# Routing of a two-expert MoE block by sums of powers of two, with row numbers counted on TensorE, and a jump-back hint held in a register

## The reference

```python
h = _layernorm(x) * (1 + ca) + sa
g = sigmoid(h @ Wg.T + bg);  a = sigmoid(h @ Wd.T + bd);  v = h @ Wv.T + bv
x = x + ga * (scan(h_t = a_t * h_{t-1} + (1 - a_t) * v_t) * g)
h = _layernorm(x) * (1 + cb) + sb
probs = softmax(h @ gate_w.T + gate_b);  top 2 of 8 -> dense_gate
y_e = relu(h @ w1[e] + b1[e]) @ w2[e] + b2[e]
x = x + gb * sum_e dense_gate[e] * y_e
```

## Time and profile before

| | |
|---|---|
| median of 3 runs | 443.9 us (442.91 to 444.16) |
| the profiled execution | 442.52 us, of which the span is 440.7 us |
| busy, share of the span | DVE 88%, PE 83%, ACT 73%, POOL 43% |
| mean granted clock of TensorE | 0.922 of full speed |
| chain that ended last, by engine | PE 58%, DVE 27%, issue 8% |

### The profile page before, as it was taken

The page is one execution under the profiler, slowest core; times in us unless marked ns, Lnnn a source line. Parts: engine busy times, 40 slices in busy tenths (PEclk is TensorE's granted clock), DMA queues, the critical chain, the costliest instruction groups (busy, mean ns, idle before and its releaser), DMA issues.

```text
span 440.7 us, 15289 instructions
## 1 busy us (share of the span) xinstructions
PE 366.2 (83%) x4679; PEld 316.8 (72%) x4680; DVE 386.4 (88%) x1099; ACT 320.0 (73%) x992; POOL 188.7 (43%) x213
## 2 busy tenths in 40 slices
PE   1859889789787683489999999999999999999660
PEld 1435555456455562489999999999999999989660
DVE  4989999989998999699999899999999998888660
ACT  1445999688979550188988888889888888877530
POOL 8023303376678477884333243333333334324321
PEclk9986999989999655599999999999999999999895
DMA  7813643131223243563333333333333333232200
GB/s 217 223 48 106 202 146 106 48 128 73 92 90 126 93 163 147 147 197 106 84 98 84 95 94 100 87 88 86 87 86 91 94 85 87 66 81 73 64 11 7
DMA packets 45941, 45.27 MB, mean 103 GB/s; under 512 B 5934, under 2 KB 40575, under 8 KB 45874
## 3 DMA queue, kind: packets, MB, share of 16 engines
q1 hardware_dynamic: 38208, 27.28, 23.1%
q0 software_dynamic: 6592, 16.92, 10.6%
q10 hardware_dynamic: 1074, 0.23, 0.3%
HBM read 24.52 MB, written 20.81 MB: 103 GB/s over the span
## 4 chain that ended last, share of the span: by engine, by line
PE 58%; DVE 27%; issue 8%; DMA 2%; ACT 1%; SPq 1%; POOL 0%; POOLq 0%; ACTq 0%; DVEq 0%
PE bank L1513 8%; PE bank L1514 8%; PE bank L1515 8%; PE bank L1530 8%; PE bank L1531 7%; PE bank L1529 7%; DVE xn L921 3%; PE bank L1526 2%; DVE hs L935 2%; PE bank L1488 2%; PE bank L1370 2%; DVE st L865 2%; DVE u L931 2%; DVE st L859 2%; DVE pay L944 2%
## 5 line engine op out<-in xcount | busy, mean ns | idle before, releaser
L755 ACT ACTIVATE xs<-bank,b1col 128x128 f32<-128x128 f32 x624 | 165.2, 415 | 26.4 <-PE bank L1515 25.5
L590 POOL DMA_INDIRECT out_dram<-tg,midx x78 | 81.9, 1049 | 150.9 <-DVE tg L1299 135.0
L1513 PE MATMUL bank<-xh,w1hi 128*128 128x128 f16 x624 | 109.9, 223 | 6.6 <-issue 3.7
L1529 PE MATMUL bank<-w2hi,xs 128*128 x624 | 112.7, 219 | 0.0
L1530 PE MATMUL bank<-w2hi,w2f 128*128 x624 | 112.6, 219 | 0.0
L1531 PE MATMUL bank<-w2lo,xs 128*128 x624 | 112.6, 219 | 0.0
L1515 PE MATMUL bank<-xh,w1lo 128*128 128x128 f16 x624 | 109.9, 222 | 0.0
L1514 PE MATMUL bank<-xl,w1hi 128*128 128x128 f16 x624 | 109.9, 223 | 0.0
L1279 DVE TENSOR_TENSOR w2f<-xs 128x1024 f16<-128x1024 f32 x78 | 95.6, 1225 | 2.7
L561 POOL DMA_INDIRECT sorted_rows<-pay,idx x64 | 69.1, 1080 | 28.2 <-issue 18.7
L1277 DVE CAST xs<-xs 128x1024 f16<-128x1024 f32 x78 | 54.7, 701 | 13.1 <-ACT xs L755 9.5
(11 more groups left out here) (232 smaller groups left out, 654.2 us busy)
## 6 DMA issues: line engine op xcount, KB each, us to landing
xs<-sorted_rows SPq DMA_DIRECT2D x78, 130.0 KB
xs<-sorted_rows SPq DMA_DIRECT2D x78, 64.0 KB
sorted_rows<-padt SPq DMA_DIRECT2D x5, 582.0 KB, 5.3
w2f<-in_L_ffn_w_dram SPq DMA_DIRECT2D x4, 512.0 KB, 3.9
xs<-in_L_ffn_w_dram SPq DMA_DIRECT2D x4, 512.0 KB, 3.8
xs<-in_L_attn_x_dram SPq DMA_DIRECT2D x3, 512.0 KB, 8.7
out_dram<-tg,midx POOLq DMA_INDIRECT x78
sorted_rows<-pay,idx POOLq DMA_INDIRECT x64, 2.7
```

The lines of the kernel that those rows point to most:

```text
L590: pool.indirect_dma_start(out_rows, bass.IndirectOffsetOnAxis(midx[k][:, t:t + 1], 0), yout[k][:, t, :], None, bounds_check=TOK - 1, oob_i ...
L755: ins = act.activation(hf[e][:, cc, t * P:(t + 1) * P], bank[2 * e + cc // 2][:, o:o + P], ACT.Relu, bias=b1col[:, bass.ds(ex[t][e] * HC + ...
L1513: pe.matmul(o, whi, xh[n % 2][:, rows], start=True, stop=False)
L1529: pe.matmul(o, hh[n % 2][e][:, cc, rows], whi, start=False, stop=False)
```

## The change

Routing: the two choices are coded as powers of two (`desc` holds 128, 64, ..., 1 in place of 8, 7, ..., 1). Their sum `key` names the pair, and `OH` compares it with a table `key_of`. The arithmetic that made a pair's number, its direction and its start (`cmax`, `cmin`, `elo`, `tri`, `q`, `aq`, `way`, `start`) goes. PE's count adds the start of each list by one more matmul with `list_base`, and takes backward and forward lists in separate matmuls of 14 lists each, the former with negative masks; the product with `OH`, summed, is the row number itself. POOL's setup makes the new tables. The loop is written by hand: a register `final` is 1 in the last turn and 0 before, and the prefetch hint takes its outcome from it.

```diff
+        @contextmanager
+        def tile_loop(eng, turns):
...
+            nc.regs_mov(it, PEEL)
+            nc.br(head, engines=on)
+            with nc.body(head, valid_engines=on):
+                now = nc.snap(it, min_val=PEEL, max_val=MAX_TURNS - 1)
+                eng.reg_alu(final, now + 1, turns, ALU.is_ge)
+                place = eng.mark_branch_hint_location()
+                yield now
+                nc.regs_alu(it, it, 1, ALU.add)
+                eng.br_lt(it, turns, on_true=head, on_false=behind).branch_hint(place, final)
+            nc.switch_bb(behind)
...
-            with nc.Fori(PEEL, turns, engines=[pe.engine], hint_back_edge=True) as it:
+            with tile_loop(pe, turns) as it:
...
-            mark(pool.iota(cnti[:, E:2 * E], pattern=[[-1, E]], base=E, channel_multiplier=0))
+            for e in range(E):
+                mark(pool.memset(desc[:, e:e + 1], float(1 << (E - 1 - e))))
+            mark(pool.memset(list_base[:, :], 0.0))
...
+                mark(pool.tensor_scalar(key_of[:, first:first + hi], desc[:, 0:hi], float(1 << (E - 1 - hi)), None, ALU.add))
...
-                mark(dve.tensor_tensor(m["cmax"], m["c1"], m["c2"], ALU.max))
-                mark(dve.tensor_tensor(m["cmin"], m["c1"], m["c2"], ALU.min))
-                done = marked(dve.tensor_tensor(m["isl"], m["c1"], m["c2"], ALU.is_gt))
-                yield
-
-                dve.wait_ge(dve_step, done)
-                mark(dve.tensor_scalar(m["elo"], m["cmax"], -1.0, E * (E - 1) / 2 + E - MID, ALU.mult, ALU.add))
-                done = marked(dve.scalar_tensor_tensor(out=m["tri"], in0=m["cmin"], scalar=1.0 - 2 * E, in1=m["cmin"],
-                                                       op0=ALU.add, op1=ALU.mult))
-                yield
-                dve.wait_ge(dve_step, done)
-                done = marked(dve.scalar_tensor_tensor(out=m["q"], in0=m["tri"], scalar=0.5, in1=m["elo"],
-                                                       op0=ALU.mult, op1=ALU.add))
-                yield
+                done = marked(dve.tensor_tensor(m["key"], m["c1"], m["c2"], ALU.add))
+                mark(dve.tensor_tensor(m["isl"], m["c1"], m["c2"], ALU.is_gt))
+                yield
+
                 dve.wait_ge(dve_step, done)
                 after(dve, rank_ready, sg - 1)
-                dve.tensor_tensor(OH[sg % 2][:, 0:n, :], over_tiles(q_iota[:, :], n, PAIRS), wide(m["q"], PAIRS),
+                dve.tensor_tensor(OH[sg % 2][:, 0:n, :], over_tiles(key_of[:, :], n, PAIRS), wide(m["key"], PAIRS),
                                   ALU.is_equal).then_inc(oh_ready, 1)
-                mark(dve.scalar_tensor_tensor(out=m["aq"], in0=m["q"], scalar=-1.0, in1=m["q"],
-                                              op0=ALU.mult, op1=ALU.max))
-                done = marked(dve.tensor_scalar(m["way"], m["q"], 0.0, 0.5, ALU.is_gt, ALU.subtract))
...
-                done = marked(dve.tensor_reduce(m["pos"], prod[:, 0:n, :], AX_X, ALU.add))
...
+                with nc.allow_low_precision(reason="one whole number below 2 ** 17 and zeros"):
+                    dve.tensor_reduce(idx[:, t0:t0 + n], prod[:, 0:n, :], AX_X, ALU.add).then_inc(idx_ready, 1)
...
-                pe.matmul(rank, upper[:, :], ohf, start=True, stop=False)
-                for t in range(1, n):
-                    pe.matmul(rank[:, t * PAIRS:], ones_bf[:, :], ohf[:, 0:(n - t) * PAIRS], start=False, stop=False)
...
+                pe.matmul(rank, ones_bf[:, :], list_base[:, :].unsqueeze(1).to_broadcast([P, n, PAIRS]),
+                          start=True, stop=False)
+                for lists, above, every in ((slice(0, HALF_LISTS), minus_upper, minus_ones),
+                                            (slice(HALF_LISTS, PAIRS), upper, ones_bf)):
+                    pe.matmul(rank[:, :, lists], above[:, :], OH[sg % 2][:, 0:n, lists], start=False, stop=False)
+                    for t in range(1, n):
+                        pe.matmul(rank[:, t:, lists], every[:, :], OH[sg % 2][:, 0:n - t, lists], start=False, stop=False)
```

More of the change, by code:

```diff
@@ L13 @@
-from contextlib import ExitStack
+from contextlib import ExitStack, contextmanager
 from itertools import chain
@@ L71 @@
 PAD_J = 3
-MID = (PAIRS - 1) / 2
+HALF_LISTS = PAIRS // 2
 SEEN0 = SGT * PAIRS
@@ L183, in adaln_moe_kernel @@
         small = [{n: sb(f"r_{n}{k}", [P, SGT]) for n in
-                  ("m1", "c1", "c2", "s", "p1", "p2", "cmax", "cmin", "elo", "tri",
-                   "q", "aq", "start", "way", "signed", "isl", "dp", "low", "pos")} for k in range(2)]
+                  ("m1", "c1", "c2", "s", "p1", "p2", "key", "isl", "dp", "low")} for k in range(2)]
         pair_iota = sb("pair_iota", [P, PAIRS])
-        q_iota = sb("q_iota", [P, PAIRS])
+        key_of = sb("key_of", [P, PAIRS])
         off_of = sb("off_of", [P, PAIRS])
         dir_of = sb("dir_of", [P, PAIRS])
-        low_of = sb("low_of", [P, PAIRS])
+        back = sb("back", [P, PAIRS])
+        span_of = sb("span_of", [P, PAIRS])
+        list_base = sb("list_base", [P, PAIRS], BF16)
         OH = [sb(f"OH{k}", [P, SGT, PAIRS], BF16) for k in range(2)]
@@ L386, in experts @@
             return [[code % E, code // E % E], [code // E ** 2 % E, code // E ** 3]]
+        @contextmanager
+        def tile_loop(eng, turns):
+            on = [eng.engine]
+            head, behind = (f"tiles_{eng.engine.name}_{part}" for part in ("head", "behind"))
+            it = nc.alloc_registers(f"turn_{eng.engine.name}", engines=on)
+            final = eng.alloc_register(f"final_{eng.engine.name}")
+            nc.regs_mov(it, PEEL)
[8 more added lines that the diff above has]
+            nc.switch_bb(behind)
         block = ctx.enter_context(nc.Block())
@@ L462, in _ @@
                     reload_y(it, k - BUFS)
-            with nc.Fori(PEEL, turns, engines=[sp.engine], hint_back_edge=True) as it:
+            with tile_loop(sp, turns) as it:
                 for k in range(BUFS):
@@ L501, in _ @@
                 mark(pool.memset(t[:, :], 1.0))
+            for t in (minus_ones, minus_upper):
+                mark(pool.memset(t[:, :], -1.0))
             mark(pool.memset(seen[:, :], 0.0))
@@ L521, in _ @@
+            mark(pool.tensor_scalar(back[:, :], pair_iota[:, :], float(HALF_LISTS), None, ALU.is_lt))
+            mark(pool.tensor_scalar(span_of[:, :], pair_iota[:, :], -float(HALF_LISTS), None, ALU.add))
             join()
-            mark(pool.tensor_scalar(q_iota[:, :], pair_iota[:, :], -MID, None, ALU.add))
-            mark(pool.tensor_scalar(row_mid[:, :], row_mid[:, :], -(UNIT - 1) / 2, None, ALU.add))
+            mark(pool.tensor_scalar(dir_of[:, :], back[:, :], -2.0, 1.0, ALU.mult, ALU.add))
@@ L536, in _ @@
+            join()
+            mark(pool.tensor_tensor(off_of[:, :], off_of[:, :], back[:, :], ALU.subtract))
+            join()
+            mark(pool.tensor_scalar(off_of[:, :], off_of[:, :], float(UNIT), None, ALU.mult))
+            join()
+            mark(pool.tensor_tensor(off_of[:, :], off_of[:, :], span_of[:, :], ALU.add))
             for hi in range(1, E):
@@ L598, in _ @@
                     write_tile(it, k)
-            with nc.Fori(PEEL, turns, engines=[pool.engine], hint_back_edge=True) as it:
+            with tile_loop(pool, turns) as it:
                 for k in range(BUFS):
@@ L780, in _ @@
                     last = last_turn(act)
-            with nc.Fori(PEEL, turns, engines=[act.engine], hint_back_edge=True) as it:
+            with tile_loop(act, turns) as it:
                 for k in range(BUFS):
@@ L1066, in place_rows @@
                 dve.wait_ge(dve_step, done)
-                done = marked(dve.tensor_reduce(m["pos"], prod[:, 0:n, :], AX_X, ALU.add))
-                yield
-                dve.wait_ge(dve_step, done)
-                done = marked(dve.scalar_tensor_tensor(out=m["signed"], in0=m["pos"], scalar=-(TOK - 1) / 2, in1=m["way"],
-                                                       op0=ALU.add, op1=ALU.mult))
-                yield
-                dve.wait_ge(dve_step, done)
-                dve.scalar_tensor_tensor(out=idx[:, t0:t0 + n], in0=m["signed"], scalar=2.0, in1=m["start"],
-                                         op0=ALU.mult, op1=ALU.add).then_inc(idx_ready, 1)
+                with nc.allow_low_precision(reason="one whole number below 2 ** 17 and zeros"):
+                    dve.tensor_reduce(idx[:, t0:t0 + n], prod[:, 0:n, :], AX_X, ALU.add).then_inc(idx_ready, 1)
                 yield
@@ L1324, in _ @@
                     last = last_turn(dve)
-            with nc.Fori(PEEL, turns, engines=[dve.engine], hint_back_edge=True) as it:
+            with tile_loop(dve, turns) as it:
                 for k in range(BUFS):
```

29 lines of the change are left out of this document (15 added, 14 removed).

## The result

The changed kernel takes 437.76 us (median; 436.07 to 437.98 in four runs) beside 444.03 for the kernel before: a ratio of 0.9868, 95% interval 0.9829 to 0.9907. Timed again beside other runs of the kernel before it came to 0.9882 (0.9823 to 0.9940). The times of one kernel spread with the granted clock: the ten runs of the changed one took 434.26 to 440.97 us at mean clocks of 0.906 to 0.928, the 51 of the kernel before that stand beside the experiments 441.07 to 447.33 us at 0.900 to 0.928. So ratios, which leave out the runs over 1.5% above the fastest of their kernel, carry 0.3 to 0.7% on either side, and where less is asked I compare stretches of the profiled executions. It is faster by some 6 us, inside the range of 429.5 to 438.5, but only 0.7 us from its upper end; the forecast was 433.0, with 430.5 to 435.5 as its own range.

What follows compares the result with a forecast made beforehand. DVE's routing chains bound the kernel up to the table, plus PE's 3.35 us hole behind the loop. 442.5 - 6.7 (routing) - 4.3 (exit) + 0.2 (register) = 431.7, as a median 433 us; own range 430.5 to 435.5, wide range 429.5 to 438.5.

Steps and rivals of the forecast that it cites:

- Exit: PE behind the loop: a right hint removes the 3.35 us hole at the exit; gain 4.3 us, ends nothing and 4.7.
- The reading as code not fetched: PE's 3.35 us hole behind the loop: instructions not yet fetched because the hint named the other way; no row names a fetch.
- exit unchanged: Rival at the loop's exit: the register hint is not taken or the hole has another cause; 437.4 us, chance 0.14.
- the Trainium skill's rule on taken branches: Loop: sequential prefetch, taken branches out of the window wait; jumps back should cost, exit be free, so no 4.3 us gain.
- Jumps: Loop heads on PE: three jumps back under 0.5 us each; the register instruction costs 0.05 each time, 0.2 us in all.
- the rival of the other side: Loop's three jumps back: hint armed late or not at all, 4.3 us each; 446 us, or 450 without the exit; chance 0.06.
- Routing behind the last scan: Last `choose` and `place_rows` steps up to the table: 0.3 + 1.0 + 0.2 = 1.5 us gained, the table still last.
- Routing in the turns: Shorter `choose` and `place_rows` on DVE up to the last scan: 5.6 us, of which 5.2 taken; low end 3.
- the overlap: Turns: DVE's residual comes some 2 us after `r`, covering PE's lateness of about 0.9 us, so DVE does not wait.
- DVE waiting for PE's transposes: Sign of a wrong forecast: DVE waits for PE's transposes of `r` in turns 7, 10 and 12, PE having become the bound.
- no half clock in turn 9: Rival in the turns: PE idles less, so it is not let down to half clock; gains 1.8, 431.2 us, chance 0.09.
- PE and ACT swallow the routing's gain: Rival in the turns: PE and ACT are nearly full, so routing gains only 3 us; 436.8 us, chance 0.11.

Runs made afterwards that it cites:

- the hint alone: Kernel before with the loop's prefetch hint taken from a register and nothing else changed; 440.19 us, ratio 0.9908.
- routing only: Changed kernel with the loop of the kernel before, its jump back statically hinted as taken; 436.62 us, ratio 0.9842.
- always out: Changed kernel with the loop's hint set to 'falls through' in every turn, so wrong at each jump back; 437.66 us, ratio 0.9830.
- second profile: Changed kernel unaltered, timed and profiled once more beside other runs of the kernel before; 438.31 us, ratio 0.9882.
- before, shifted: Kernel before with 156 increments of a semaphore that nobody waits for added to PE's program; 448.78 us, ratio 1.0119.
- filled: Changed kernel with 12 unread products ahead of PE's wait for the logits' input, in groups up to the third last; 433.45 us, ratio 0.9739.
- short filled version: Changed kernel with unread products ahead of the logits' wait only up to group 11, and 20 more in three later PE waits; 433.15 us, ratio 0.9761.

## Why the prediction was right, and where its size was off

*Exit.* Mechanism and size held: 4.3 forecast, 4.2 measured, and 4.2 for the hint alone by the same stretch. The reading as code not fetched was called a reading; the hole that follows the length of the program and the instruction packets now show it. The rival "exit unchanged" fell with it, though its 437.4 came nearest of all to the time. I had taken the Trainium skill's rule on taken branches (Runtime: NRT & Kernel Launch, section Instruction fetch mechanics) as a rule against the reading; it says nothing of hints and only speaks of targets out of the fetched window. A turn of the loop is some 465 instructions of PE, and no packet of q8 came between 361 and 406 us in the changed kernel, so these jumps back did not put the rule to the test. One remark in the prediction was worth more than I made of it: that the code had moved, "so that the hole may have moved in any case". It did. The longer counts alone shrink the hole to 0.75 us and take back the exit's loss (the run "routing only"); the hint's 4.2 us are therefore not added to the routing's, since each would have got them without the other.

*Jumps.* They did not miss; the rival of the other side fell, and by "always out" it could not have happened through a wrong hint at all. The register was put at 0.2 us for the loop; 0.8 was measured (51.18 to 51.95; 52.12 with the hint alone). Over both tables the loop takes 51.18 to 51.60 us with the static hint and 51.95 to 52.67 with the register.

*Routing behind the last scan.* 1.5 forecast, 1.3 in both profiles of the changed kernel. The table still comes last.

*Routing in the turns: the term that was mis-sized.* I took 5.2 us; in the execution timed first it was 3.0, in the second profile 5.2. The step that failed is the overlap: I wrote that the residual has some 2 us of other work ahead, so that DVE does not wait for PE's transposes of `r`, and that the half clock of turn 9 moves with DVE "but no further". DVE's work is shorter as costed, but its waits for these transposes grew. From turn 2 to 15 (us, from windows and waits):

```
                        turns   DVE     DVE waits for PE's   half
                                busy    transposes of r
before                  111.60  104.68  3.7                  1
before, shifted         113.04  104.64  5.2                  5
after                   108.65   99.66  6.5                  3
after, second profile   106.42   99.59  4.4                  2
always out              110.16   99.64  8.0                  5
filled                  105.27   99.68  3.1                  1
```

DVE's work falls by 5.0 us in each kernel with the new routing; what reaches the time goes by the waits. And the waits go by PE's half clock: in the profiles of the two tables of stretches each such wait between turns 2 and 15 of over 1.1 us ends within 2 us of the end of a stretch at half clock. The old routing loses less to such stretches (113.0 with five against 111.2 to 111.6 with one) than the new one (110.2 with five, 106.4 to 109.5 with three, 106.4 with two, and 105.3 to 105.8 with one, with fillings). That fits with PE's waits for DVE, which took up its lateness before and are now mostly gone; but five stretches were met in one execution of either only. The profiles of the new routing without fillings have two to five such stretches, those of the old one have one, but for the five of the shifted one. That the new routing is let down more often is not shown by this: the granted clocks of the timed runs are alike in the two kernels. What the filled runs show is that with the clock kept up the new routing gives more. The longer count's own part stays open; with one stretch in each DVE waits 3.1 us in the filled kernel and 3.7 before, so none is seen there. DVE waiting for PE's transposes, named in the prediction as the sign that PE had become the bound, is there, in turns 9, 10, 11, 13 and 14; of the turns 7, 10 and 12 that I had named only in one. My rival "no half clock in turn 9" had the sign wrong. "PE and ACT swallow the routing's gain" (3 us in the turns, 436.8) had the cause nearest, through PE.

*Not foreseen.* Tiles 0 to 8 take 0.6 (second profile) to 1.4 us more. In the first profile 0.9 of it is PE's wait for tile 8, whose rows were 3.81 us on the way; in the second that is absent, so it belongs to the execution. Tiles 0 to 3 (to the transposes of tile 4) take 20.6 to 20.8 us in the versions of the new routing without fillings and 20.4 to 20.5 with the old one; that they start earlier into the long stretch at half clock is a reading, and the short filled version, with 20.65 us though the clock was back at 173.3, does not bear it out. POOL's longer setup stayed hidden.

The sum of the first profile: -0.5 (start) - 3.0 - 1.3 + 1.4 + 0.2 + 0.8 - 4.2 = -6.6, which is the 6.5 between the spans but for rounding; the forecast's was -5.2 - 1.5 - 4.3 + 0.2. That the range held, by 0.7 us, owes something to its width, which was drawn to hold the rivals too; in the second profile the spans are 8.2 us apart. What stays open is why the clock falls where it does: the filled versions show that work in PE's waits keeps it up, not how much is needed.

## What to carry to other kernels

When work is taken off the engine that sets a stretch, look at what the second engine's clock will do, not only at its busy time: here 5.0 us of work went from DVE, and in the execution timed first 2 of them were lost again in waits for a PE at half clock, where the old routing lost less to the same half clock. The price of leaving a hinted loop hangs on where the program's length puts the exit, so an edit far ahead of it can take or give 4 us; before a gain at an exit is credited to an edit, shift the program by itself. And where the times of one kernel spread by more than the question, compare stretches between the same instructions.

## What the runs showed of the hardware that was not expected

- A jump back that is hinted as falling through cost PE no more than one hinted rightly (0.39 to 0.43 us at the heads against 0.40 to 0.47), while an exit hinted as a jump cost up to 3.44 us.
- PE stops until 3.3 to 3.95 us after such an exit (3.30, 3.50, 3.77, 3.86 and 3.95 in five kernels), wherever that is in the code; the hole is what is left of it behind the work at hand.
- The granted clock fell to 0.50 behind a stretch in which PE was busy 12.07 of 13.70 us, and stayed at 1.00 over one with 35.51 of 37.50 and, in another execution, over one with 47.50 of 54.60, so these rows do not tell why it fell.
- Increments of a semaphore as instructions of their own on PE took 0.15 us each (50 in 7.55 us). With 106 of them in two waits of 4 us each, turn 2 came 6.4 us late.
